# A two-layer graph network on one core: another instruction order in the steps of layer 0 and between the layers, a far loop without waits, and five gathers left out

## The reference, cut to what matters

```
# layer 0: mean over the incoming edges, a linear layer, ReLU, residual, layer norm
mean = segment_sum(x[src], dst) / max(deg, 1)          # x itself where deg is 0
x    = layernorm(x + relu(concat([x, mean]) @ W.T + b))
# layer 1: attention over the incoming edges, with typed weights
Q, K, V = x @ W_Q[type], x @ W_K[type], x @ W_V[type]  # type of the node, 4 of them
score   = (Q[dst] . (K[src] @ W_edge[edge_type])) * mu[edge_type] / sqrt(128)
out     = segment_sum(V[src] * softmax_over_dst(score), dst)
x       = layernorm(x + out)
```

## Time and profile before

| | |
|---|---|
| median of 3 runs | 3727.59 us (3725.5 to 3731.58) |
| the profiled execution | 3697.22 us, its span 3695.4 us |
| mean granted TensorE clock | 0.839 of full speed |
| layer 0, steady steps | from about 131 to 1334 us of the span |
| between the layers | 1334 to 1364 us |
| layer 1 | 1364 us to the end |

### The profile page before, as it was taken

How to read it: one execution, slowest core, us unless ns; L and a number is a source line. 1 busy time by engine, 2 the same in 40 slices (tenths; PEclk the granted TensorE clock), 3 DMA queues, 4 the chain that set the end, 5 groups by cost and what they waited for, 6 DMA issues and landing times.

```text
span 3695.4 us, 38864 instructions
## 1 busy us (share of the span) xinstructions
PE 2551.0 (69%) x13692; PEld 1754.7 (47%) x13692; DVE 1530.9 (41%) x4283; ACT 1124.1 (30%) x2072; POOL 2372.2 (64%) x2400
## 2 busy tenths in 40 slices
PE   1688888888888861666666666666676666666667
PEld 0355555555555541444444444444444444444445
DVE  8466666666666620222222222222222222222223
ACT  3333444444444420222222222222222222222222
POOL 6656667676666617566666666666666666666662
PEclk9799999999999985777777777777777777777778
DMA  4233344443444313233333333333333333333331
GB/s 135 64 98 115 107 130 120 119 120 107 120 120 120 112 68 107 72 96 96 97 97 96 97 97 96 97 97 96 97 97 97 97 97 96 96 97 97 97 97 43
DMA packets 195810, 369.81 MB, mean 100 GB/s; under 512 B 62177, under 2 KB 126509, under 8 KB 189347
## 3 DMA queue, kind: packets, MB, share of 16 engines
q0 software_dynamic: 112432, 281.92, 27.5%
q1 hardware_dynamic: 76679, 82.09, 6.7%
q10 hardware_dynamic: 6508, 3.33, 0.3%
HBM read 299.89 MB, written 67.30 MB: 99 GB/s over the span
## 4 chain that ended last, share of the span: by engine, by line
PE 38%; another core or an unknown queue 20%; issue 19%; ACT 14%; DVE 8%; ACTq 1%; DMA 0%; DVEq 0%; POOLq 0%; POOL 0%; SPq 0%
PE banks L715 8%; ACT work L1090 5%; PE banks L872 4%; PE banks L886 4%; PE banks L901 3%; PE banks L708 3%; ACT work L1098 3%; ACT picks L1007 2%; PE banks L738 2%; DVE sums L1269 2%; PE banks L771 1%; PE banks L908 1%; PE banks L866 1%; PE banks L776 1%
## 5 line engine op out<-in xcount | busy, mean ns | idle before, releaser
L655 POOL DMA_INDIRECT ring<-kv_table,src_n x1264 | 1207.9, 956 | 625.9 <-issue 368.8
L650 POOL DMA_INDIRECT ring<-x_part_rows,work x512 | 538.0, 1051 | 249.2 <-issue 138.4
L886 PE MATMUL banks<-identf,ring 128*128 128x128 f32 x1264 | 242.9, 319 | 646.5 <-ACT work L1098 458.2
L1007 ACT ACTIVATE picks<-banks 128x392 bf16<-128x392 f32 x800 | 396.6, 499 | 730.0 <-PE banks L708 646.7
L715 PE MATMUL banks<-sums,picks 128*128 128x385 bf16 x2450 | 617.6, 335 | 0.4 <-ACT picks L1007 0.4
L886 PEld LDWEIGHTS banks<-identf,ring 128*128 128x128 f32 x1264 | 169.4, 162 | 698.9 <-ACT work L1098 506.4
L1090 ACT ACTIVATE work<-banks,negmax 128x2048 f32<-128x2048 f32 x98 | 193.0, 1969 | 905.9 <-issue 668.4
L1098 ACT ACTIVATE work<-banks 128x512 f32<-128x512 f32 x392 | 213.0, 598 | 816.1 <-remote 689.1
L1467 DVE SCALAR_TENSOR_TENSOR sums<-sums,corr,banks 128x128 f32<-128x128 f32 x98 | 34.0, 347 | 936.5 <-remote 928.9
L1448 DVE TENSOR_REDUCE largest<-banks 128x1 f32<-128x2048 f32 x98 | 224.6, 2292 | 468.9 <-PE banks L872 252.3
L872 PE MATMUL banks<-work,queries 128*128 128x512 f32 x784 | 412.2, 674 | 4.1 <-issue 4.1
(11 more groups left out here) (279 smaller groups left out, 2785.7 us busy)
## 6 DMA issues: line engine op xcount, KB each, us to landing
kv_table<-ring SPq DMA_DIRECT2D x49, 1024.0 KB
ring<-kv_table,src_n POOLq DMA_INDIRECT x1264
ring<-x_part_rows,work POOLq DMA_INDIRECT x512
sums<-kv_table,src_n POOLq DMA_INDIRECT x304
x_part_rows<-sums SPq DMA_DIRECT2D x7, 675.5 KB, 4.5
src_n<-x_part_rows,work POOLq DMA_INDIRECT x256
sums<-x_rows SPq DMA_DIRECT2D x51, 64.0 KB, 1.9
x_rows<-ring SPq DMA_DIRECT2D x49, 64.0 KB
```

The lines of the kernel that those rows point to most:

```text
L650: pool.indirect_dma_start(near[k % RUNS][:, j, :], None, part_dram, bass.IndirectOffsetOnAxis(ap=col_ids[:, first + j:first + j + 1], axis ...
L655: pool.indirect_dma_start(kv_ring[u][:, j, :], None, table, bass.IndirectOffsetOnAxis(ap=of, axis=0)).then_inc(l1_rows[2 * u + j // RUN], 16)
L886: tr = pe.transpose(bank[KEY_BANK[g]][:, j * P:(j + 1) * P], kv_ring[k.u][:, g * 4 + j, 0:D], identf[:, :])
L1007: act.activation(picked[:, par, :, c * NW:(c + 1) * NW], bank[c % 2][:, 0:KEYS].rearrange("p (h w) -> p h w", w=NW), ACT.Copy).then_inc(pi ...
```

## The change

Six edits, in all engines' lists:

1. In a step of layer 0 TensorE's pieces stand later in the loop over `h`: `node_sum` at 6 instead of 3, the late tile's pieces and the second `run_sum` one later, `transpose_mean` at 36 instead of 35, `first_product` at 42 instead of 40.
2. VectorE makes the second group of one-hots of the next step, `hot(i + 1, par, 1)`, behind `join_parts`, instead of at the end of the step before, ahead of `join_parts`.
3. ScalarE takes the early tile's `deviation` ahead of the last `take` of the step, not behind it.
4. Between the layers the pieces of tile 47 and of tile 48 alternate on TensorE and ScalarE, and VectorE takes `mean` and `relu` of tile 48 ahead of `copy_low` of tile 47. For this, tile 48 has its own PSUM bank (`front`: bank 4, not 5).
5. GpSimd issues the first eight gathers of layer 1 ahead of the far loop, and the loop no longer waits for TensorE's scores: `far_gathered` counts up instead of being taken back.
6. The five padding columns of the last block aren't gathered, and TensorE waits for the rows that are.

```
+        def front(tile):
+            return bank[4] if tile.t == TILES - 1 else bank[5]
...
# gpsimd
-                gate(pool, far_score_ps, it + 1)
-                pool.inc_swdge_sem([far_gathered], [32], mode="sub")
-
-            far_sweep(pool, lambda i: None, far, lambda i: None)
             pool.wait_ge(keys_ready, 4)
             for b in range(NBLK):
                 if b >= SLOTS1:
                     pool.wait_ge(values_ps, b - SLOTS1 + 1)
-                for j in range(COLS):
+                for j in range(min(COLS, NCOLS - b * COLS)):
+                    if b == 0 and j == RUN:
+                        far_sweep(pool, lambda i: None, far, lambda i: None)
                     gather(b % SLOTS1, j, key_idx[:, b * COLS + j:b * COLS + j + 1])
...
# tensor, transpose_x
-                pe.wait_ge(q_copied, tile.t + 1)
-                pe.transpose(bank[5][:, 0:P], x_tile[tile.k], identf[:, :]).then_inc(xT_ps, 1)
+                if tile.t < TILES - 1:
+                    pe.wait_ge(q_copied, tile.t + 1)
+                else:
+                    pe.wait_ge(runs_vec, 3 * (ND - 2))
+                pe.transpose(front(tile)[:, 0:P], x_tile[tile.k], identf[:, :]).then_inc(xT_ps, 1)
...
# tensor, l0
-                    if h == 3 and i > 0:
+                    if h == 6 and i > 0:
                         node_sum(i - 1)
                     if late:
-                        if h == 8:
+                        if h == 9:
                             transpose_typed(late)
...
-                        if h == 35:
+                        if h == 36:
                             transpose_mean(early)
-                        if h == 40:
+                        if h == 42:
                             first_product(early)
...
# tensor, behind the sweep
-            late_part(tile(TILES - 2))
-            last = tile(TILES - 1)
+            first, last = tile(TILES - 2), tile(TILES - 1)
+            transpose_typed(first)
             transpose_x(last)
+            project_keys(first, added(ND))
             transpose_mean(last)
+            project_values(first)
             first_product(last)
+            project_queries(first)
+            low_keys(first)
+            high_keys(first)
             late_part(last)
...
# tensor, transpose_keys
-                        pe.wait_ge(l1_rows[2 * k.u + g // 2], (k.fill + 1) * (16 * RUN))
+                        rows_of = min(RUN, NCOLS - k.b * COLS - g // 2 * RUN)
+                        pe.wait_ge(l1_rows[2 * k.u + g // 2], (k.fill * RUN + rows_of) * 16)
...
# tensor, far
-                gate(pe, far_staged, it + 1)
-                pe.wait_ge(far_gathered, 32)
+                gate(pe, far_gathered, it * 32 + 32)
...
# scalar, l0
-                if early:
-                    deviation(early)
+                    if early and c == 14:
+                        deviation(early)
...
# vector, l0
                 if i > 0:
                     join_parts(i - 1, (i - 1) % 2)
+                if i + 1 < ND:
+                    hot(i + 1, (i + 1) % 2, 1)
...
                     normalise_x1(early)
-                if i + 2 < ND:
-                    hot(i + 2, i % 2, 1)
...
# vector, behind the sweep
-            copy_low(tile(TILES - 2))
             last = tile(TILES - 1)
             mean(last, added(ND))
             relu(last)
+            copy_low(tile(TILES - 2))
             normalise_x1(last)
             copy_low(last)
```

30 lines of the change are left out of this document (16 added, 14 removed).

## The result

The changed kernel is slower: 3753.26 us (median of 14 runs, 3734.83 to 3795.19) against 3725.4 us (14 runs, 3715.33 to 3731.58) of the kernel before, a ratio of 1.0075 with a 95% interval of 1.0059 to 1.0091. I had predicted 3610 us. The profiled execution after took 3772.37 us, its span 3770.5 us. An execution more than 1.5% above the fastest of its kernel counts as slow and is left out of the ratios (3795.19 us is one).

The account below looks back on a forecast made before the run. TensorE was taken to bound layer 0, GpSimd close behind. Gains of 110 (layer 0), 3 (between layers), 0 (layer 1's start) and 4.6 us (last block) made 118 us off 3727.6: 3610 us, range 3590 to 3656.

Parts of the forecast that it names:

- The node sum and TensorE's other waits: Layer 0: of TensorE's 166.7 us of waits 38 us stay, 7 us of them at the node sum.
- terms of 129 us: Layer 0: what TensorE alone would give back, 2.7 us a step, for a step of 21.5 us.
- The step that failed: Layer 0: a 21.5 us step clears GpSimd's 21.2 us; 0.3 to 0.4 us a step lost, 16 us.
- 110 us won: Layer 0's gain: 129 us less 16 us, taken as 110 us, bounds 85 and 129.
- Rival C: Layer 0: TensorE's signals held, 5.1 us a step, 3852 us; decides from 2.5 us a step; chance 0.04.
- my own signs of being wrong: Key projection takes over the node sum's wait, gathers of 1.2 us become common, or picks wait for nothing named.
- Rival A: Layer 0: GpSimd becomes the bound, gathers stretch another 1 us a step; gain 70 us, 3650 us; chance 0.16.
- Between the layers: Tiles 47 and 48: TensorE's 2.64 us of idling for VectorE goes; gain 3 us, bounds 0 and 6.
- The start of layer 1: 80 gathers end some 5 us earlier, far chain starts 10 us later; taken as 0, bounds -10 to +18.
- rival B: Start of layer 1: the far chain's signals are held while gathers run, 18 us later, 3628 us; chance 0.12.
- The last block: End of layer 1: five gathers fewer, ScalarE goes on at 3634.5; gain 4.6 us, bounds 3 and 7.

Follow-up runs that it names:

- fewer_new: The changed kernel with six gathers instead of eight in each layer 0 batch behind the first three (sums partly wrong): 3485.28 us, ratio 0.9428 to the kernel before.
- steps_only: The kernel before with only the new order in layer 0's steps: 3746.10 us, ratio 1.0156 to the kernel before.
- seam_only: The changed kernel with layer 0's steps in the old order again: 3677.72 us, ratio 0.9946 to the kernel before.
- changed_again: The changed kernel unaltered, run once more on another chip: 3725.12 us, ratio 1.0059 to the kernel before.
- new_spaced: The changed kernel with a 128x256 memset behind each gather of layer 0: 3314.19 us, ratio 0.9897 to the kernel before.
- narrow_new: The changed kernel with gathers of half the bytes from layer 0's fourth batch on (sums partly wrong): 3766.13 us, ratio 1.0129 to the kernel before.
- the relays: The changed kernel with ScalarE passing TensorE's slot signal to GpSimd, or the gathers' signals to TensorE: 3745.54 us (1.0119) and 3719.82 us (1.0050).
- seven_filled: The changed kernel with seven gathers instead of eight in a batch, a 128x64 memset behind each (sums partly wrong): 3516.13 us, ratio 0.9517 to the kernel before.
- drain_new: The changed kernel, but GpSimd issues a batch of gathers only when the one before has landed: 3742.42 us, ratio 1.0110 to the kernel before.
- seam_product: The kernel of seam_only with `transpose_mean` at 36 instead of 35 and `first_product` at 42 instead of 40: 3743.34 us, ratio 1.0104 to the kernel before.

## Why the prediction was wrong, point by point

**The node sum and TensorE's other waits: right.** The waits of `fewer_new` are what I had worked out for TensorE alone: 3.8 us at the node sum (I had 7), 9.2 us at `transpose_mean` (47 x 0.2 = 9), none in the table at `first_product` (7), 3.4 us at the key projection (14). The step fell by 24.2 - 20.7 = 3.5 us, more than the 2.7 us of the sum; where the other 0.8 us come from wasn't worked out. These are the terms of 129 us; with six gathers they are worth 174 us (last gather of layer 0 at 1091.8 instead of 1266.3).

**The step that failed: "That is 0.3 us above the 21.2 us that GpSimd needs", with 0.3 to 0.4 us lost between the two engines.** I treated GpSimd's 3.0 us of pause as spare time that can be taken away, and put the loss between the two engines at 16 us. In its place the runs show late signals of TensorE: with all sixteen gathers in a step they stall it, and GpSimd then stops for 4.6 to 11 us; with twelve gathers and the same order they are gone (4.9 us of "remote" at the picks, step 20.7 us). In no run with all gathers on the three chips that have late signals is the mean step of layer 0 shorter than 24.2 us. In place of 110 us won, the last gather of layer 0 is 45.3 us later in `steps_only` than in `seam_only`, on one chip: 155 us off, 3.3 us a step.

**Rival C was the case**, with its mechanism, its place (the picks) and its point of decision (2.5 us a step); only its price was too high (5.1 us a step for 3.3). Its sign, picks that wait for nothing that the profile names, stood among my own signs of being wrong. I gave it 0.04, because sixteen unbroken gathers around 306 us had passed without harm. That quiet step was less like the other than I wrote. Its sixteen gathers took 23.0 us, several of them 1.4 to 1.9 us long; those of the step at 131 us took 21.1 us, and TensorE lost 6.3 us at picks in it (2.57, 1.97 and three of 0.5 to 0.6 us), of which I quoted one. And one quiet step outweighed the evidence of the long stage: in layer 1 of the kernel before, 92 of GpSimd's waits are named "remote", 3.1 us each, one behind every sixteen unbroken gathers. The last row (4.59 us, "remote") and GpSimd's 3.17 us there are the same thing that I should have priced for layer 0. The Trainium skill (SBUF — State Buffer, Who interferes with whom) says that TensorE never waits on anyone at the SBUF's ports. That is a rule on ports and not on signals: no run here shows a port as the cause, and ScalarE's 271.3 us above are waits for TensorE's signal, which the rule doesn't speak of.

**Rival A** (gathers stretched by more than 1 us a step) did not come: the mean of a gather in layer 0 is 1.04 us in `changed_again` and 1.06 us in the kernel before.

**Between the layers: right.** I had 3 us. In `seam_only` the first gather of layer 1 and the rows below are the timeline's:

```profile
1360.36 0.95 POOL L658 DMA_INDIRECT ring<-kv_table,src_n  x1 [78.97 <-SPq L519]
1404.66 3.25 PE L897 MATMUL banks<-identf,ring 128*128 128x128 f32 x16 [21.25 <-issue]
1457.24 2.29 DVE L1461 TENSOR_REDUCE largest<-banks 128x1 f32<-128x2048 f32 x1 [53.16 <-remote]
1490.44 0.95 POOL L658 DMA_INDIRECT ring<-kv_table,src_n  x1 [26.62 <-PE banks L919]
3605.31 0.95 POOL L658 DMA_INDIRECT ring<-kv_table,src_n  x1 [3.20 <-remote]
3621.12 2.06 ACT L1111 ACTIVATE work<-banks 128x512 f32<-128x512 f32 x4 [2.01 <-PE banks L897]
```

VectorE starts behind `l1_start` at 1360.22 instead of 1363.57: 3.35 us. The seam itself gave 3.7 us, as the last node sum of layer 0 started 0.34 us later.

**The start of layer 1: the term was mis-sized.** I took 0. The 80 gathers ended at 1463.83 instead of 1475.78, 12 us earlier, of which the seam gave 3.4: I had counted only the 6.88 us of idle time, not the copy and the far loop's own two gathers. TensorE's first transposes came 12.8 us later (1404.66 for 1391.89; I had 10), and its first score 16 us later. That cost little: GpSimd waited 26.62 us behind the stream instead of 25.09. The sixth block starts at 1490.44 instead of 1500.87, 7 us gained beyond the seam. Here the end of the gathers counted, not how far TensorE had come, and the reason is again late signals. The first row below is the end of the first score in the kernel before, the others are the same place in `new_spaced`, on the chip without "remote" waits:

```profile
1408.96 2.08 PE L872 MATMUL banks<-work,queries 128*128 128x512 f32 x2 [4.05 <-issue]
1354.71 2.74 PE L889 MATMUL banks<-work,queries 128*128 128x512 f32 x6
1357.48 2.29 DVE L1467 TENSOR_REDUCE largest<-banks 128x1 f32<-128x2048 f32 x1 [8.66 <-PE banks L889]
```

In the kernel before, the score was done at 1411.04, and VectorE started on it at 1441.21, and SyncE at 1441.20: 30 us late, with GpSimd's gathers running all the while. In `new_spaced` it was done at 1357.45 and taken 0.03 us later. So of the 49.87 us that rival B quotes about 30 were a held signal; the rest lay ahead of the end of the score. This one row could have warned of rival C. Rival B's 18 us for the far chain did not come.

**The last block: right in kind.** From the start of its gathers to the end it takes 3677.6 - 3605.31 = 72.3 us instead of 79.1: 6.8 us, near the upper bound of 7, not 4.6. ScalarE's copy comes 15.8 us behind the first gather instead of 22.8, so ScalarE's 3634.5 (18.2 us behind it), which I took as the floor, was none. In all, edits 4 to 6 were worth 19 us where I had put 7.6.

**What stays open.** Which part of GpSimd's issuing holds the signals. Not the bytes (`narrow_new`), not the two semaphores (the relays). Pause or density isn't settled. On the chips with late signals, twelve and fourteen gathers a step at 20.7 and 21.3 us (`fewer_new`, `seven_filled`) and sixteen at 24.2 us went free or nearly so, 1.5 us a gather and more; sixteen in 23.0 us, as in layer 1, didn't. But `drain_new` speaks against both: with 1.7 us a gather and longer pauses than the kernel before, it still had 91 us of "remote" at the picks. A third possibility, that it matters where TensorE's pieces fall within GpSimd's batches, fits how little `seam_product` moved, and was not tried. Why one chip has no late signals at all was not tried either.

## What to carry to other kernels

An engine's short, regular pauses need not be spare time. Before a change closes them, look in the same profile for a stage where they are closed, and take its waits named "remote" as the price: here closing them went with late signals, though it is not shown that the pauses themselves let the signals through. That stage was layer 1. Where several edits share one sum, run them apart: the loss of edits 1 to 3 hid the 19 us that edits 4 to 6 gain (`seam_only`, 0.5% faster than the kernel before), and a control with less load on the suspected engine (six gathers for eight) told in one pair of runs that the reasoning on the other engines was sound. Compare only within a chip: the kernel before took between 3348 and 3725 us.

## What the runs showed of the hardware that was not expected

- On three chips TensorE's semaphore signals reach ScalarE, VectorE and GpSimd late and together while GpSimd issues indirect gathers densely: with waits of up to 5.2 us at the picks of the changed kernel, and, in the kernel before, with a first score of layer 1 that VectorE and SyncE got 30 us late. Some were let out 1.2 us after the stream ended, others in the middle of it. In the first place shown, signals between ScalarE and VectorE were not late: VectorE's statistics ended at 1205.32 and ScalarE began on them at 1205.36, and VectorE went on 0.04 us after ScalarE.
- On a fourth chip the two kernels that ran there show none of it: 20.1 us for a block of layer 1 against 22.99 us and 23.2 us on the others, and the same signal of the first score within 0.03 us. The kernel before takes 3348 us there, against 3697 to 3725 us.
- A gather of 128 rows mostly costs GpSimd 0.96 us (the longest in layer 0 up to 2.2 us), whether a row has 386, 772 or 1024 bytes; a memset of 128x64 between two gathers adds only 0.04 us, since it fits into the 0.30 us there.
- The granted clock follows the stalls: 0.98 in layer 0 before, 0.93 in the profile after, 1.00 where TensorE was busy 98% of the time.
